# Two extra PSUM copies on ScalarE, two group-norm products on GpSimd and an early weight load in a fused RWKV-6 and local-attention kernel

## The reference, cut to what matters

```python
xn = _layernorm(x)
# recurrent block (s)
xx = shift(xn) - xn
t5 = tanh((xn + xx * tmx) @ maa_w1).reshape(B, T, 5, 32)
m  = einsum('btfe,fec->fbtc', t5, maa_w2)
xw, xk, xv, xr, xg = (xn + xx * (tm_f + m[f]) for f in 0..4)
r, k, v, g = xr @ Wr, xk @ Wk, xv @ Wv, silu(xg @ Wg)
decay = exp(-exp(tdecay + tanh(xw @ td_w1) @ td_w2))
y_t = r_t @ (S + u * k_t v_t^T);  S = decay_t * S + k_t v_t^T
yn = (y - mean) / sqrt(var + eps) * ln_w + ln_b      # per head of 64
s = (yn * g) @ Wo
# gate: two transformer layers on xn (local attention of window 512, then GEGLU)
for l in range(2):
    x = x + local_attention(rotary(l2norm(shift(x) @ wqkv[l]))) @ wo[l]
    x = x + (a * gelu(g)) @ w2[l] + b2[l]            # a, g = norm(shift(x)) @ w1[l] + b1[l]
out = x_in + s * silu(x)
```

## Time and profile before

| what | value |
|---|---|
| time, median of 2 runs | 4637.25 us (4630.76 to 4643.74) |
| the profiled execution's own time | 4666.49 us |
| its span, slowest core (core 6) | 4665.0 us |
| its fastest core (core 0) | 4596.0 us |
| busy: PE, DVE, ACT, POOL | 2409.9, 1895.3, 711.5, 64.6 us |

### The profile page before, as it was taken

One profiled execution on the slowest core, in us unless ns is written; L12 is line 12 of the kernel. 1 busy time (PEld: TensorE's weight loads), 2 busy tenths in 40 slices (PEclk: granted clock), 3 DMA queues, 4 the chain that ended last, 5 costly groups with the idle time before them and its releaser, 6 DMA issues.

```text
span 4665.0 us, 39106 instructions; the slowest of 8 cores (4596.0 to 4665.0 us)
## 1 busy us (share of the span) xinstructions
PE 2409.9 (52%) x11904; PEld 1135.0 (24%) x11904; DVE 1895.3 (41%) x4429; ACT 711.5 (15%) x1430; POOL 64.6 (1%) x58
## 2 busy tenths in 40 slices
PE   1445445566312152544454798664444446997750
PEld 0223223233211121211111343322111112343320
DVE  4555555444577712333435321122433444311243
ACT  2112112111000010121221111001122222111010
POOL 0000000000000000000000000000000000000000
PEclk9656556677655586666556899887656557898875
DMA  5100000300222123000002132440000030223314
GB/s 121 46 10 10 19 10 10 64 19 27 64 45 57 34 91 46 0 1 0 0 11 46 39 72 59 98 71 0 0 1 0 1 50 14 57 58 71 83 66 166
DMA packets 181642, 190.74 MB, mean 41 GB/s; under 512 B 77664, under 2 KB 139488, under 8 KB 181408
## 3 DMA queue, kind: packets, MB, share of 16 engines
q1 hardware_dynamic: 139648, 131.67, 9.2%
q0 software_dynamic: 41792, 56.59, 8.1%
HBM read 184.00 MB, written 60.82 MB: 52 GB/s over the span
## 4 chain that ended last, share of the span: by engine, by line
PE 44%; DVE 27%; issue 9%; ACT 8%; DMA 8%; DVEq 1%; POOL 1%; SPq 0%; ACTq 0%; POOLq 0%
PE ps L1313 12%; PE ps L1383 7%; PE ps L1004 4%; PE pw L1104 4%; ACT arena_b L1111 4%; DVE arena_b L421 3%; PE pw L563 3%; PE ps L396 2%; DMA arena_b<-w2p 2%; DMA arena_f<-s_d 2%; PE ps L500 2%; PE pw L1175 2%; DVE arena_f L746 2%; PE pw L1130 1%; DVE arena_b L385 1%
## 5 line engine op out<-in xcount | busy, mean ns | idle before, releaser
L1313 PE MATMUL ps<-arena_b 128*128 128x512 bf16 x2816 | 658.2, 399 | 68.5 <-DVE arena_b L1328 68.5
L1313 PEld LDWEIGHTS ps<-arena_b 128*128 128x128 bf16 x2816 | 285.3, 102 | 447.2 <-issue 184.0
L1383 PE MATMUL ps<-arena_b 128*128 128x512 bf16 x1408 | 323.7, 396 | 115.1 <-DMA arena_b<-w2p 115.1
L1116 DVE TENSOR_TENSOR arena_b<-arena_b,arena_f 128x128 bf16<-128x128 bf16 x448 | 130.2, 292 | 509.1 <-ACT arena_b L1111 508.1
L1328 DVE SCALAR_TENSOR_TENSOR arena_b<-ps,arena_f,arena_b 128x512 bf16<-128x512 f32 x176 | 131.6, 750 | 497.9 <-ACT arena_b L1323 445.0
L1104 PE MATMUL pw<-arena_b 64*128 64x128 bf16 (+1 forms) x448 | 185.7, 419 | 281.6 <-ACT arena_b L1111 280.2
L1004 PE MATMUL ps<-arena_b 128*128 128x512 bf16 x768 | 187.3, 404 | 178.2 <-DVE arena_b L995 146.4
L1111 ACT ACTIVATE arena_b<-pw 128x128 bf16<-128x128 f32 (+1 forms) x448 | 195.0, 437 | 397.3 <-PE pw L1104 397.2
L1383 PEld LDWEIGHTS ps<-arena_b 128*128 128x128 bf16 x1408 | 142.0, 101 | 296.8 <-issue 163.4
L1323 ACT ACTIVATE arena_b<-ps,arena_f 128x512 bf16<-128x512 f32 x176 | 120.9, 687 | 568.6 <-PE ps L1313 565.0
L421 DVE SCALAR_TENSOR_TENSOR arena_b<-ps,arena_f 128x256 bf16<-128x256 f32 x320 | 153.1, 478 | 128.5 <-PE ps L416 128.5
(11 more groups left out here) (172 smaller groups left out, 3070.0 us busy)
## 6 DMA issues: line engine op xcount, KB each, us to landing
h_d<-arena_b SPq DMA_DIRECT2D x176, 128.0 KB, 1.8
arena_b<-h_d SPq DMA_DIRECT2D x16, 1408.0 KB, 6.4
arena_f<-x SPq DMA_DIRECT2D x32, 512.0 KB, 5.0
arena_b<-w1p POOLq DMA_DIRECT2D x4, 3072.0 KB, 23.9
arena_b<-w2p POOLq DMA_DIRECT2D x4, 2816.0 KB, 25.4
arena_b<-w1p POOLq DMA_DIRECT2D x4, 2560.0 KB, 29.2
arena_b<-rq_d SPq DMA_DIRECT2D x16, 512.0 KB, 5.0
s_d<-arena_f SPq DMA_DIRECT2D x16, 512.0 KB, 2.7
```

The source lines that it names most:

```text
L1116: p.emit("vector", lambda v, ab_=ab_, oo=oo, mko=mko, msk=msk: v.tensor_tensor(ab_[:, oo + mko: oo + mko + 128], ab_[:, oo + mko: oo + mko ...
L1313: last = t.matmul(pb.ap()[:], wb[:, k * 1536 + (2 * pi + agi) * 128: k * 1536 + (2 * pi + agi) * 128 + 128], z1[:, k * T + tt4 * 512: k * ...
L1383: last = t.matmul(pb.ap()[:], wb2[:, k * C + ctO * 128: k * C + ctO * 128 + 128], hs[:, k * 512:(k + 1) * 512], start=(k == 0), stop=(k == ...
```

## The change

Four edits. First, in the m loop of both passes ScalarE copies the PSUM bank to a float32 buffer (`msb`, two of them), which VectorE then reads; the bank is freed by the copy. Second, in the r loop ScalarE copies r to a float32 buffer (`rrb`, two of them), which both VectorE instructions then read. Third, in phase 2 the product with `lnw_rep` and the sum with `lnb_rep` are done by GpSimd. Fourth, three of the eight row groups of layer 0's `wqkv` and all of its `wo` are loaded to fixed places of the arena behind phase 1 (`prefetch_ffn0`), and `attn_stage(0)` loads the other five groups; layer 1 loads `wqkv` in two DMAs.

```diff
@@ setup
+        self.wq_lo = self.ab.t.ap()[:, 46900:46900 + 3 * 1536]
+        self.wo2 = self.ab.t.ap()[:, 51520:51520 + 4 * C]
@@ phase1, m loop
+                    msb = msb2[ct % 2]
+                    p.emit("scalar", lambda sc, pb=pb, msb=msb: sc.activation(
+                        msb, pb.ap()[:, 0:TS], AF.Copy),
+                        waits=[(sm, None)] + G(("msb", ct % 2)), incs=[(sa, 1)])
+                    SG(("pk", ct % 2), sa)
-                        zb, pb.ap()[:, 0:TS], self.vecs[nmv][:, ct:ct + 1],
+                        zb, msb, self.vecs[nmv][:, ct:ct + 1],
                         xx[:, ct * TS:(ct + 1) * TS], ALU.add, ALU.mult),
-                        waits=[(sm, None)] + G(("zbb", ct % 2)), incs=[(sv, 1)])
-                    SG(("pk", ct % 2), sv)
+                        waits=[(sa, None)] + G(("zbb", ct % 2)), incs=[(sv, 1)])
+                    SG(("msb", ct % 2), sv)
@@ phase1, r loop
+                    rrb = rrb2[ct % 2]
+                    p.emit("scalar", lambda sc, pb=pb, rrb=rrb: sc.activation(
+                        rrb, pb.ap()[:, 0:TS], AF.Copy),
+                        waits=[(sm, None)] + G(("rrb", ct % 2)), incs=[(sa, 1)])
+                    SG(("pk", ct % 2), sa)
-                        fRQ[:, ct * TS:(ct + 1) * TS], pb.ap()[:, 0:TS], e1, ALU.mult),
-                        waits=[(sa, None), (sm, None)] + G(("fRQ", ct)), incs=[(sv, 1)])
+                        fRQ[:, ct * TS:(ct + 1) * TS], rrb, e1, ALU.mult),
+                        waits=[(sa, None)] + G(("fRQ", ct)), incs=[(sv, 1)])
-                        rkub, pb.ap()[:, 0:TS], self.vecs["u_"][:, ct:ct + 1],
+                        rkub, rrb, self.vecs["u_"][:, ct:ct + 1],
-                    SG(("pk", ct % 2), sv)
+                    SG(("rrb", ct % 2), sv)
@@ prefetch_ffn0, called between phase1 and phase2
+        p.emit("gpsimd", lambda gp: gp.dma_start(
+            out=self.wq_lo.rearrange("p (g n) -> p g n", g=3),
+            in_=d["wqkv"][0].rearrange("(g p) n -> p g n", p=128)[:, 5:8, :]),
+            waits=list(self.p1_done), incs=[(s, 16)])
+        p.emit("gpsimd", lambda gp: gp.dma_start(
+            out=self.wo2.rearrange("p (g n) -> p g n", g=4),
+            in_=d["wo"][0].rearrange("(g p) n -> p g n", p=128)),
+            waits=[], incs=[(s, 16)])
@@ phase2
-            p.emit("vector", lambda v: v.tensor_tensor(ysb, sqb, self.lnw_rep, ALU.mult),
-                   waits=[(sv, None), (sl, None), (self.sem("p2_lnr"), 32)], incs=[(sv, 1)])
-            p.emit("vector", lambda v: v.tensor_tensor(sqb, ysb, self.lnb_rep, ALU.add),
-                   waits=[(sv, None)], incs=[(sl, 1)])
+            p.emit("gpsimd", lambda g_: g_.tensor_tensor(ysb, sqb, self.lnw_rep, ALU.mult),
+                   waits=[(sv, None), (sl, None), (self.sem("p2_lnr"), 32)], incs=[(sl, 1)])
+            p.emit("gpsimd", lambda g_: g_.tensor_tensor(sqb, ysb, self.lnb_rep, ALU.add),
+                   waits=[(sl, None)], incs=[(sl, 1)])
@@ attn_stage
-            wqkv_sb = self.ab.alloc(8 * 3 * INNER)
-            wo_sb2 = self.ab.alloc(4 * C)
+            wq_hi = self.ab.alloc(5 * 3 * INNER)
+            wo_sb2 = self.wo2
+                in_=d["wqkv"][l].rearrange("(g p) n -> p g n", p=128)[:, 0:5, :]),
                 waits=[(sm, None), (sv, None)], incs=[(sgw, 16)])
+            if l > 0:
...
+                    in_=d["wqkv"][l].rearrange("(g p) n -> p g n", p=128)[:, 5:8, :]),
+                    waits=[(sm, None), (sv, None)], incs=[(sgw, 16)])
...
```

More of the change, by code:

```diff
@@ L350, in phase1 @@
         fG = fKK
+        msb2 = [self.af.alloc(TS) for _ in range(2)]
+        rrb2 = [self.af.alloc(TS) for _ in range(2)]
         sv = self.sem("p1_v")
@@ L511, in tile_pass @@
                     SG(("teb", ct % 2), sa)
[L512 to L516 removed]
+                    rrb = rrb2[ct % 2]
[3 more added lines that the diff above has]
+                    SG(("pk", ct % 2), sa)
+                    p.emit("vector", lambda v, ct=ct, rrb=rrb, e1=e1b[ct % 2]: v.tensor_tensor(
+                        fRQ[:, ct * TS:(ct + 1) * TS], rrb, e1, ALU.mult),
+                        waits=[(sa, None)] + G(("fRQ", ct)), incs=[(sv, 1)])
+                    p.emit("vector", lambda v, ct=ct, rrb=rrb: v.scalar_tensor_tensor(
+                        rkub, rrb, self.vecs["u_"][:, ct:ct + 1],
                         kf[:, ct * TS:(ct + 1) * TS], ALU.mult, ALU.mult),
                         waits=[(sv, None)] + G(("rkub",)), incs=[(sv, 1)])
[L519 removed]
+                    SG(("rrb", ct % 2), sv)
                     SG(("e1b", ct % 2), sv)
@@ L627, in phase1, with prefetch_ffn0 @@
         self.af.reset(m); self.ab.reset(mb)
+    def prefetch_ffn0(self):
+        p, d = self.p, self.dram
+        s = self.sem("p4_gw")
+        p.emit("gpsimd", lambda gp: gp.dma_start(
[6 more added lines that the diff above has]
+            waits=[], incs=[(s, 16)])
     def phase2(self, parts=31):
@@ L903, in attn_stage @@
             self.ab.reset(m4a)
-            wqkv_sb = self.ab.alloc(8 * 3 * INNER)
-            wo_sb2 = self.ab.alloc(4 * C)
+            wq_hi = self.ab.alloc(5 * 3 * INNER)
+            wo_sb2 = self.wo2
             p.emit("gpsimd", lambda gp, l=l: gp.dma_start(
-                out=wqkv_sb.rearrange("p (g n) -> p g n", g=8),
-                in_=d["wqkv"][l].rearrange("(g p) n -> p g n", p=128)),
+                out=wq_hi.rearrange("p (g n) -> p g n", g=5),
+                in_=d["wqkv"][l].rearrange("(g p) n -> p g n", p=128)[:, 0:5, :]),
                 waits=[(sm, None), (sv, None)], incs=[(sgw, 16)])
[L910 to L913, removed]
+            if l > 0:
+                p.emit("gpsimd", lambda gp, l=l: gp.dma_start(
+                    out=self.wq_lo.rearrange("p (g n) -> p g n", g=3),
+                    in_=d["wqkv"][l].rearrange("(g p) n -> p g n", p=128)[:, 5:8, :]),
+                    waits=[(sm, None), (sv, None)], incs=[(sgw, 16)])
+                p.emit("gpsimd", lambda gp, l=l: gp.dma_start(
+                    out=wo_sb2.rearrange("p (g n) -> p g n", g=4),
+                    in_=d["wo"][l].rearrange("(g p) n -> p g n", p=128)),
+                    waits=[], incs=[(sgw, 16)])
             tabs_raw = {}
@@ L955, in attn_stage @@
             xbnd = self.ab.alloc(8 * NW)
+            assert self.ab.off <= 46900, f"attn allocs {self.ab.off} hit prefetch region"
             for rwi in range(3):
@@ L1003, in qkvmm @@
                             for k in range(8):
+                                wsrc = (wq_hi[:, k * 1536 + wh * 512: k * 1536 + (wh + 1) * 512]
+                                        if k < 5 else
+                                        self.wq_lo[:, (k - 5) * 1536 + wh * 512: (k - 5) * 1536 + (wh + 1) * 512])
                                 last = t.matmul(pb.ap()[:],
                                                 zwin[:, k * 512 + ts_ * 128: k * 512 + ts_ * 128 + 128],
-                                                wqkv_sb[:, k * 1536 + wh * 512: k * 1536 + (wh + 1) * 512],
+                                                wsrc,
                                                 start=(k == 0), stop=(k == 7))
@@ L1608, in build_nc @@
         b.phase1()
+    if phases > 4:
+        b.prefetch_ffn0()
     if phases > 2:
```

2 lines of the change are left out of this document (1 added, 1 removed).

## The result

The changed kernel took 4705.76 us (median of 11 runs, 4681.40 to 4771.25) beside 4642.19 us for the kernel before in the same comparison. The ratio is 1.013, 95% interval 1.0088 to 1.0172: slower by 41 to 80 us, most likely by 60. I had forecast 29 us. The direction and the range (4635 to 4712 us) hold, the range by only 6 us, and the forecast is about half of what was measured. The change is under 2%, to which the prediction gave 0.92. Ratios with an interval, and the medians given for the last two experiments, leave out runs in which the cores of one die ran longer at a lower granted clock (here the one of 4771.25 us).

What follows compares the result with a forecast made beforehand. No engine bounds the whole: the stages stand one behind the other, each with its own limit. Terms -10 + 27 + 21 + 5 - 14.5 + 0.5 = +29 us on the median 4637.25 gave 4667 us, 0.6% slower, range 4635 to 4712.

Steps and rivals of the forecast that it cites:

- rival (a): Phase 2: GpSimd reads two different inputs at twice the time, +82 us instead of +21, 4727 us; chance 0.13, whole or good part.
- The bounds of 0 to 16: Start of phase 2: 0 us later if the new loads are served fully behind the chunk loads, 16 if fully ahead.
- Sharing by halves: Start of phase 2: new loads and chunk loads share DMA engines, stretching the 9.70 us wait by at most as much again.
- my bound of 31: r loop of pass 1: upper bound for the 64 r copies, 64 x 0.48 us.
- The circle: r loop: matmuls, VectorE and head sums wait on each other, 3.74 us a turn; a copy inside adds 0.47 us.
- the two ends: m loop, each pass: +0.47 us at the start for the first copy, 1.1 us sooner at the end; net -10 us.
- The head of phase 4: TensorE's wait for loads before layer 0: 6.2 us go without wo, 8.3 with less wqkv; -14.5 us, bounds -10 to -18.
- Rival (d): Head of phase 4: four small tables set the wait, not the bytes of the weights; 4681 us, chance 0.08.
- Rival (b): r loop: the r copies are hidden, since TensorE would find the bank free earlier; 4640 us, chance 0.07.
- (c): m and r loops: VectorE gets faster without PSUM reads, 105 us less if its instructions took half; 4562 us, chance 0.02.
- both terms with wide bounds: GpSimd's products in phase 2, +21 us (0 to +82), and the early load at phase 2's start, +5 us (0 to 16).

Runs made afterwards that it cites:

- the last two experiments: Kernel before with m copies, head sums one block late and layer 0's load at chunk 4: 4588.1 us, ratio 0.991; same without m copies: 4585.2 us, ratio 0.989.

## Why the prediction came out as it did

**GpSimd's products: +21 forecast, +39.3 measured; the step that failed.** That the difference is paid in full, since VectorE and TensorE both wait for it, was right: it is in the chain. The duration was not. I took L775, "since it is the only one of GpSimd at this shape", and kept a bound of twice the time for two different inputs. The row answered for equal inputs only: 2.338 us against 1.892, 24% more and far from twice, so rival (a) is wrong as a price and right as a mechanism. The rule of the Trainium skill that I had set beside it (GPSIMD Engine Reference, section 3.1, ratio 1.96) gave 2.40 us and +38; the runs give 2.338 / 1.226 = 1.91 and +39.3. Here the Trainium skill was the better source, and the trace's disagreement that I had noted came from the equal inputs. I had also put the hand-overs at nothing: with the small rest of the chunk they are 3.7 us. Of the 18.3 us missed, 32 x (2.338 - 1.892) = 14.3 are the duration and 4 this.

**The early load at the start of phase 2: +5 forecast, +14.4 measured.** The bounds of 0 to 16 held, the choice inside them was poor. "Sharing by halves would stretch the 9.70 us by at most as much again" is where it fails: the wait went from 9.70 to 23.68 us, by more than as much again. That is near the 16 us estimated for new loads served ahead of all of SP's; in which order they were served is not shown.

**The r copies: +27 forecast, about +32 measured** (8 x (4.17 - 0.18) from the tile table; +31.4 alone, just past my bound of 31). The circle and its +0.48 were right; the 0.09 us by which the first of the eight matmuls starts later were not in it. The rule of the Trainium skill that I weighed there (VectorE: DVE Perf Modes, Rules for kernel authors) offers such a copy if many operations follow; in float32 at 128x256 it made none of the three groups shorter, as rows 2 had said.

**The m copies: -10 forecast.** In the changed kernel the two ends come to +0.61 and -1.40 us a tile in pass 1 (forecast +0.47 and -1.1), with -3.3 us in pass 2: 8 x 0.79 + 3.3 = 9.6 us. Both ends were worked out nearly right, but that the number comes out is in part luck: alone the same edit gave 7 us, all but one of them in pass 2, since forty matmuls a tile were 0.63 us longer (8 x 0.63 = 5 us), and in the changed kernel they were 0.31 longer. The prediction had no term for that.

**The head of phase 4: -14.5 forecast, -13.7 measured.** Right, and by the mechanism given: the last small table landed 8.7 us behind the last weights before and lands 8.2 us behind them now (means of eight cores), so the whole gain is in the weights. Rival (d), by which the bytes of the weights wouldn't matter, falls. Rival (b) falls by the chain, and (c) by the three groups.

**The sum.** +29 forecast, +63.6 measured. The 34.6 us missed are 18.3 of GpSimd, 9.4 of the start of phase 2, 7.6 of phase 1 (27.9 - 3.3 beside 17), and 0.8 at the head, less 0.9 in phase 3 and 0.5 that I had given to layer 1. That the range held is owed to its width: its upper bound took in half of the way to (a), and the time came to within 6 us of it. All the large misses have one sign: at both terms with wide bounds I took a value near the favourable end.

## What to carry to other kernels

A row of the trace is a price only for what it really does: look at its operands (here one buffer given twice) before it is used for an instruction of the same shape. Moving work off a busy engine gains nothing where the other engines wait for it in a closed circle; first look for the order that opens the circle (here two small matmuls one block later, 26 us, 3 of them by the clock). A prefetch is to be issued where nobody waits for a transfer: the same loads cost 14 us behind phase 1 and nothing beside chunk 4.

## What I had not expected of the hardware

GpSimd took 1892 ns for a float32 128x1024 operation of two inputs that are one buffer, and 2338 ns if they are two, product or addition alike. Loads on the software queue (2.23 MB in 928 packets) held up those on the hardware queue by about 14 us, though they were issued at the same moment (that queue moved 4.72 MB in 7616 packets from 1217 to 1260 us, the last stores of phase 1 included); whether the size of the packets decides the share was not tried. And a tile of pass 1 that had been made 1.2 us shorter in one place grew by about as much in another: 0.47 us for the first copy, and 0.63 us because the same forty matmuls got the higher clock later (0.60 instead of 0.66 over them in the tile shown).
